# Loading and turning of the inputs put into the one order of functions, in a four-layer cross-attention kernel

## The chip, the cores and the metric

One core of one Trainium2 chip runs the kernel. The metric is the device time of one execution in microseconds (us); the time before is the median of three runs.

## The reference

```python
# x (8, 256, 256), ctx (8, 64, 128), position ids (1, 256), token types (8, 256), media mask (8, 64)
x = L0(x, ctx, W_mem, W_gate, b_gate, norm_w)          # fuse: x attends to ctx @ W_mem.T, a gate, rms norm
x = L1(x, ctx, token types, positions, weights)        # two experts, 16 heads
x = L2(x, ctx, media mask, weights)                    # gated cross attention and gelu feed-forward
x = L3(x, ctx, token types, positions, weights)        # as L1, other weights

# L1 and L3:
vm[:, :-1] = (types[:, :-1] == 1) & (types[:, 1:] == 1)
h = rms_norm(x); mixed = where(vm, h @ v_qkv, h @ l_qkv)
q, k, v = heads(split(mixed)); q, k = apply_rotary(q, k, position_ids)
c = causal_attention(q, k, v); x = x + where(vm, c @ v_dense, c @ l_dense)
x = x + cross_attention(rms_norm(x) @ cq_w, ctx @ ckv_w) @ cdense_w
m = rms_norm(x)
x = x + where(vm, silu(m @ v_gate) * (m @ v_up) @ v_down, silu(m @ l_gate) * (m @ l_up) @ l_down)
```

## The kernel before

x stays on chip for all four layers, transposed: `x_all` holds, for each of the eight batch elements, 256 features (two times 128 partitions) by 256 tokens. The work is cut into small functions, each for one batch element e and for one engine: `f_scores`, `f_turn`, `f_context`, `f_gate`, `f_sum`, `f_spread` are TensorE's (PE's) parts of the fuse layer; `n0_*` is the norm ahead of q, k, v; `q`, `k`, `v`, `first_scores`, `second_scores`, `values` are attention; `crs_*` and `cross_*` the cross attention; `up`, `down` the feed-forward; `a_*` and `b_*` the third layer. Elements 8 to 15 are the same eight in the last layer. A table of times (`put(time, stage)` and a start for each element) is sorted once, and every engine walks that one order and calls its own functions; a wait on another engine's semaphore stands at the head of a function. `f_scores(0)` is such a function for element 0.

Ahead of that order there is a block of its own, the first `with nc.Block()` (lines 746 to 887):

- SyncE (SP) issues the loads of the constants (line 749), W_mem, ctx, W_gate and the eight x (750 to 754), then waits until VectorE (DVE) has made the flags and copied the table of positions, and issues the first layer's weights (`load_mot`, `load_mot_ff`, lines 696 to 719, 19 transfers).
- ScalarE (ACT) issues position ids, token types, media mask and fourteen vectors, and copies the even ones of sixteen results from PSUM (line 779).
- DVE makes one-hot rows of the positions (793 to 800), the flags `is_vis`, `media_neg` and `early` (804 to 813), and copies the odd results (818).
- GpSimd (POOL) fills constants and zeroes pads (822 to 836).
- PE waits for the constants and for W_mem, ctx and W_gate together (`w0_in`, 48), then turns W_mem (848), ctx (851) and W_gate (856), makes two 512-column products (861), turns the vectors (871), makes the table of cosines and sines (867) and turns the eight x (877, four transposes each).

The block ends for every engine when all engines have ended it. The second block then starts, PE's part with

```python
                has_early = [pe.value_load(early[0:1, e:e + 1]) for e in range(B)]
```

(line 1031), which reads eight flags into registers; `q`, `k`, `v`, `dense`, `up` and `down` branch on them. `f_memory` (1346) takes four banks for its four products, and `f_scores` (1354) waits for nothing in the first four elements. Position and one-hot rows lie in the room of `qkv`, token types in that of `gate_w` and `up_w`, so the weights can't be loaded before they are used. x waits in the room of `wq` and `wkv`.

## Time and profile before

| | us |
|---|---|
| runs, median (lowest to highest) | 1487.04 (1486.95 to 1488.25) |
| the profiled execution | 1488.56 |
| its span | 1486.7 |
| PE busy | 1399.6 (94%) |
| DVE busy | 802.2 (54%) |
| ACT busy | 494.3 (33%) |
| POOL busy | 353.1 (24%) |
| mean granted clock of PE | 0.968 |

The span is what the profile shows from the first to the last instruction; the rest of the profiled execution's own time lies around it. The busy time of PE counts a matmul as long as it takes, at whichever of its two clocks; a granted clock of 1.00 is 2.4 GHz, 0.50 is 1.2 GHz, and a mean between them says for how much of a stretch each was granted. The order of the stages in time is: the first block, the fuse layer, the first expert layer (its attention from some 100 us on), the third layer (from some 600), and the last layer (from some 980).

### The profile page before, as it was taken

What the parts mean: (1) busy time and instruction counts of PE and PEld (TensorE: products, weight loads), DVE (VectorE), ACT (ScalarE), POOL (GpSimd) and SP (SyncE); (2) the same over time, 40 slices, a digit from 0 to 9 for tenths busy, and PEclk for the clock granted to TensorE, in tenths of its full rate; (3) what the DMA queues carried; (4) which work ended last, traced back from release to release, by engine and by line L of the source; (5) the groups of instructions that cost most, each with busy time, mean ns of one, the idle gap of its engine ahead of it and who ended that gap; (6) DMA issues with size and microseconds to landing.
All of it is one profiled execution on the core that took longest, in us unless ns stands there. A gap on an engine that the chain in (4) does not pass through costs nothing.

```text
span 1486.7 us, 27033 instructions
## 1 busy us (share of the span) xinstructions
PE 1399.6 (94%) x11507; PEld 1128.6 (76%) x11507; DVE 802.2 (54%) x1494; ACT 494.3 (33%) x835; POOL 353.1 (24%) x382
## 2 busy tenths in 40 slices
PE   3997899999999999999999999988799999999997
PEld 2786577877777778888888888876578787787776
DVE  3255666756766755543233332325585676765653
ACT  1241334233233232343445334513333323423321
POOL 1033432331322121110111101214223233232110
PEclk8797999999999999999999999988899999999999
DMA  8101000000001001110000000020000000000000
GB/s 263 44 1 57 2 1 2 2 1 2 2 2 43 2 5 51 47 49 1 1 1 0 1 0 1 0 77 1 2 2 9 2 8 9 2 8 2 8 9 15
DMA packets 19761, 27.36 MB, mean 18 GB/s; under 512 B 3416, under 2 KB 15408, under 8 KB 19376
## 3 DMA queue, kind: packets, MB, share of 16 engines
q1 hardware_dynamic: 18864, 24.20, 4.9%
q8 instruction: 103, 1.69, 0.5%
q10 hardware_dynamic: 768, 1.26, 0.3%
q14 instruction: 26, 0.21, 0.0%
HBM read 23.35 MB, written 2.10 MB: 17 GB/s over the span
## 4 chain that ended last, share of the span: by engine, by line
PE 84%; DVE 8%; ACT 2%; issue 2%; POOL 1%; DVEq 0%; POOLq 0%; ACTq 0%
PE bank L1299 13%; PE bank L1324 8%; PE bank L1187 6%; PE bank L1045 5%; PE bank L1515 4%; PE row_banks L1422 4%; PE bank L1522 4%; PE bank L1479 4%; PE row_banks L1170 4%; PE row_banks L1137 3%; PE bank L1038 2%; PE bank L1106 2%; PE row_banks L1451 2%; PE row_banks L1376 2%; PE row_banks L1142 2%; PE bank L1266 2%
## 5 line engine op out<-in xcount | busy, mean ns | idle before, releaser
L1636 ACT ACTIVATE room<-bank 128x256 f32<-128x256 f32 x176 | 66.7, 384 | 230.7 <-PE bank L1299 186.9
L956 POOL TENSOR_SCALAR_AFFINE_SELECT room<-room 128x1024 f32<-128x1024 f32 x64 | 72.3, 1130 | 274.6 <-ACT room L1606 274.6
L1299 PE MATMUL bank<-room,gate_w 128*128 128x256 f32 (+1 forms) x640 | 134.0, 332 | 3.7 <-DVE room L1877 2.5
L1324 PE MATMUL bank<-room,down_w 128*128 128x256 f32 (+1 forms) x704 | 134.6, 336 | 2.5 <-DVE room L1877 2.5
L1790 DVE TENSOR_REDUCE room<-row_banks 128x4 f32<-128x512 f32 (+1 forms) x128 | 116.5, 953 | 29.2 <-PE row_banks L1142 28.0
L1299 PE MATMUL bank<-room,up_w 128*128 128x256 f32 (+1 forms) x640 | 130.9, 327 | 0.0
L1606 ACT ACTIVATE room<-row_banks 128x1536 f32<-128x1536 f32 x64 | 92.9, 1452 | 109.9 <-PE row_banks L1170 109.9
L1324 PEld LDWEIGHTS bank<-room,down_w 128*128 128x128 f32 x704 | 108.5, 191 | 20.5 <-issue 6.9
L1874 DVE SCALAR_TENSOR_TENSOR room<-room,bank 128x256 f32<-128x256 f32 x176 | 73.4, 417 | 91.0 <-ACT room L1636 90.6
L1299 PEld LDWEIGHTS bank<-room,gate_w 128*128 128x128 f32 x640 | 99.6, 190 | 23.8 <-issue 9.9
L1299 PEld LDWEIGHTS bank<-room,up_w 128*128 128x128 f32 x640 | 103.0, 191 | 8.3
L1804 DVE RECIPROCAL room<-bank 128x256 f32<-128x256 f32 x32 | 56.1, 1752 | 43.2 <-PE bank L1187 43.2
L1877 DVE TENSOR_TENSOR room<-room,bank 128x256 f32<-128x256 f32 x176 | 74.1, 421 | 6.0
L1750 DVE SCALAR_TENSOR_TENSOR room<-x_all,vec_t,room 128x256 f32<-128x256 f32 x128 | 72.5, 627 | 1.7
L1170 PE MATMUL row_banks<-room 32*128 32x256 f32 (+1 forms) x1024 | 63.5, 364 | 9.7 <-DVE room L1797 6.8
L1045 PE MATMUL bank<-room,qkv 128*128 128x256 f32 x256 | 69.9, 422 | 0.0
L1170 PEld LDWEIGHTS row_banks<-room 32*128 32x128 f32 x1024 | 49.2, 194 | 26.6 <-issue 14.3
L922 POOL TENSOR_TENSOR room<-room 128x256 f32<-128x256 f32 x32 | 23.3, 727 | 194.3 <-ACT room L1616 194.3
L1515 PE MATMUL bank<-room,up_w 128*128 128x256 f32 x256 | 64.1, 395 | 1.9 <-issue 1.9
L1137 PE MATMUL row_banks<-room 32*128 32x128 f32 (+1 forms) x1024 | 60.0, 348 | 4.5 <-DVE room L1790 4.5
L1522 PE MATMUL bank<-room,down_w 128*128 128x256 f32 x256 | 61.9, 381 | 0.0
L1422 PE MATMUL row_banks<-room,wq 128*128 128x256 f32 x256 | 61.7, 384 | 0.0
(230 smaller groups left out, 2653.3 us busy)
## 6 DMA issues: line engine op xcount, KB each, us to landing
out_x<-wq SPq DMA_DIRECT2D x8, 256.0 KB, 2.1
qkv<-in_L_xattn_v_qkv SPq DMA_DIRECT2D x2, 768.0 KB, 4.3
qkv<-in_L_xattn_l_qkv SPq DMA_DIRECT2D x2, 768.0 KB, 6.0
gate_w<-in_L_xattn_v_gate SPq DMA_DIRECT2D x2, 640.0 KB, 6.9
gate_w<-in_L_xattn_l_gate SPq DMA_DIRECT2D x2, 640.0 KB, 7.8
up_w<-in_L_xattn_v_up SPq DMA_DIRECT2D x2, 640.0 KB, 6.4
up_w<-in_L_xattn_l_up SPq DMA_DIRECT2D x2, 640.0 KB, 7.1
down_w<-in_L_xattn_v_down SPq DMA_DIRECT2D x2, 640.0 KB, 7.0
```

The costliest lines, as they stand in the source:

```text
L1045: pe.matmul(out[:, t * S:(t + 1) * S], w[:, 1, k, at + t * P:at + (t + 1) * P], y_l[:, k, :], start=(t == k == 0), stop=False, skip_group_ ...
L1137: pe.matmul(row_banks[:, j, P * i:P + S * i], q_one[e % 2][par][r, t, i * P:(i + 1) * P], k_one[e % 2][par][r, t, 0:P * (i + 1)], start=(i ...
L1170: last = pe.matmul(row_banks[:, j, S * i:S + P * i], k_one[e % 2][par][r, t, i * P:(i + 1) * P], q_one[e % 2][par][r, t, i * P:S], start=( ...
L1187: last = pe.matmul(att_bank[32 * j:32 * j + 32, at + i * P:at + S], half if of_sums else v_pad[e % 2][:, i, 8 * t + 2 * j + par, :], probs ...
L1299: last = pe.matmul(b[:, j * S + lo:j * S + hi], w[:, k, f * P:(f + 1) * P], y[:, k, lo:hi], start=(k == 0), stop=(k == KT - 1))
L1324: last = pe.matmul(ff_bank[0][:, t * S + lo:t * S + hi], down_w[:, f, t * P:(t + 1) * P], hid[:, f, lo:hi], start=(i == t == 0), stop=(i = ...
L1422: last = pe.matmul(row_banks[:, u, j * S:(j + 1) * S], wq[:, k, at:at + P], a_y[:, k, :], start=(k == 0), stop=(k == KT - 1))
L1515: last = pe.matmul(ff_bank[(u + 1) % 2][:, j * S:(j + 1) * S], w1[:, k, at:at + P], b_y[:, k, :], start=(k == 0), stop=(k == KT - 1))
L1522: last = pe.matmul(crs_bank[:, t * S:(t + 1) * S], w2[:, k, t * P:(t + 1) * P], b_hid[:, k, :], start=(k == t == 0), stop=(k == GT - 1), s ...
L1606: act.activation(probs[w % 2], row_banks[:, :, 0:3 * P], ACT.Exp).then_inc(*ATT_ACT.does(e, f"exp{w}"))
L1790: last = dve.tensor_reduce(dst, row_banks[:, :, P * i:P + S * i], X, ALU.max, negate=True)
L1877: dve.tensor_tensor(hid[:, FF_ORDER[i], :], tanh_b[:, i % 2, :], b[:, S:2 * S], ALU.mult)\
```

## The change

The first block is gone. What must come first stands ahead of each engine's walk; turning and copying x, the vectors, positions and flags are functions of the order (`x_turn`, `x_out`, `p_vec`, `p_vec_out`, `p_one_hot`, `p_trig`, `p_trig_out`, `p_seen`), with counts of their own in a new section "x" of semaphores, and whoever reads a load waits for it. In detail:

- SP's constants are loaded in two parts, 128 columns first and the other 660 after x; W_gate gets a semaphore of its own (`wg_in`). The weights wait for POOL's pads alone, which POOL zeroes first.
- ACT issues positions and vectors first, copies three results, and only then issues media mask and token types. All eight x are copied by ACT.
- Position rows lie in the room of `prob_rows`, token types and their comparison in that of `q_all` and `k_all`, no longer in the weights' room.
- `f_memory` uses two banks in turn and waits for the copies; the eight register loads stand in `q(0)`.
- The table of times is another throughout: all stages of all layers have new times and starts.

```diff
-        with nc.Block() as block:
-            @block.sync
...
-                sp.wait_ge(pads_zero, 3)
-                sp.wait_ge(pro_dve, DVE_FIRST)
-                sp.wait_ge(*evacuated("trig"))
-                load_mot(sp, mot_w[0], True)
...
             @block.tensor
             def _(pe):
-                has_early = [pe.value_load(early[0:1, e:e + 1]) for e in range(B)]
+                pe.wait_ge(const_in, 16)
+                pe.wait_ge(w0_in, 32)
+                for t in range(KT):
+                    last = pe.transpose(all_banks[0][:, t * P:(t + 1) * P], w_mem_rows[:, t, :], ident)
...
+                pe.wait_ge(pro_act, 1)
+                pe.wait_ge(pro_dve, 1)
+                for t in range(KT):
+                    pe.matmul(all_banks[2 + t], w_mem_t[:, t * P:(t + 1) * P], ctx_t[:], start=True, stop=True).then_inc(pro_pe, 1)
+                pe.wait_ge(wg_in, 16)
...
+                has_early = []
+
+                def x_turn(e):
+                    pe.wait_ge(x_in[e], 16)
+                    if e >= 2:
+                        pe.wait_ge(*X_ACT.did(e - 2, "x"))
+                    else:
+                        pe.wait_ge(*((pro_act, 3), (pro_dve, 3))[e])
...
                 def q(e):
+                    if e == 0:
+                        pe.wait_ge(*X_DVE.did(0, "early"))
+                        has_early.extend(pe.value_load(early[0:1, b:b + 1]) for b in range(B))
...
                 def f_memory(e, i):
-                    pe.matmul((att_bank, crs_bank, *ff_bank)[i][:, 0:D], ctx_t[:, 2 * i * M:2 * (i + 1) * M], w_mem_t,
+                    if i < 2:
+                        pe.wait_ge(*(X_ACT.did(0, "half"), X_DVE.did(0, "trig"))[i])
+                    else:
+                        pe.wait_ge(*F_ACT.did(0, f"m{i - 2}"))
+                    pe.matmul(f_mem_bank[i % 2][:, 0:D], ctx_t[:, 2 * i * M:2 * (i + 1) * M], w_mem_t,
...
                 def f_scores(e):
                     if e >= FS:
                         pe.wait_ge(*F_DVE.did(e - FS, "y"))
+                    else:
+                        pe.wait_ge(pro_act, 3)
+                        pe.wait_ge(pro_dve, 3)
+                    pe.wait_ge(*X_ACT.did(e, "x"))
...
             @block.scalar
             def _(act):
...
+                act.wait_ge(pro_pe, 5)
+                act.copy(w_gate_t[:, 0:2, :], two(att_bank[:])).then_inc(pro_act, 1)
+                act.dma_start(media_u8[:], media_d.rearrange("b m -> (b m)").partition_broadcast(P)).then_inc(media_in, 16)
+                act.dma_start(type_i, type_d.rearrange("b n -> (b n)").partition_broadcast(P)).then_inc(type_in, 16)
+
+                def x_out(e):
+                    act.wait_ge(*X_PE.did(e, "x"))
+                    act.copy(x_of(e), two(x_bank[e % 2][:])).then_inc(*X_ACT.does(e, "x"))
...
             @block.sync
             def _(sp):
+                sp.dma_start(const[:, 0:P], const_d[:, 0:P]).then_inc(const_in, 16)
...
+                sp.dma_start(const[:, P:C_END], const_d[:, P:C_END]).then_inc(table_in, 16)
+                sp.wait_ge(pads_zero, 3)
+                load_mot(sp, mot_w[0])
+                load_mot_ff(sp, mot_w[0])
```

Of the table, the new part for what had been the first block (times are the table's own unit, only their order counts):

```diff
+    put(-20549.8448, "x_out")
+    put(-1254.5657, "x_turn")
...
+    put(126.2479, "p_one_hot")
+    put(126.4868, "f_mem", 0)
+    put(129.8263, "p_trig")
+    put(135.5925, "f_mem_out", 0)
+    put(147.7945, "p_seen")
+    put(161.3695, "p_trig_out")
...
+LOAD_STARTS = [-532.462, -287.087, 150.884, 171.195, 367.450, 608.477, 685.585, 1377.342]
```

How the order moves is shown at three places, all of PE. A row is a line of the kernel, an operation, destination and sources, its shape and how many follow each other. The first place is the passage from the turning of x to the fuse layer. Before (L877 turns x, L1354 is `f_scores`, L1346 `f_memory`):

```order
L877 MATMUL bank<-const,wkv 128x128 x16
L746 UNCONDITIONAL_BRANCH
L1029 UNCONDITIONAL_BRANCH
L1031 TENSOR_LOAD early x8
L1354 MATMUL row_banks<-room,x_all 128x64 x8
L1346 MATMUL bank<-room,ctx_t 128x256
```

Now (L945 turns x, L951 the vectors, L1297 is `f_scores`, L1285 `f_memory`, L959 the table of cosines and sines):

```order
L945 MATMUL bank<-const,wq 128x128 x12
L951 MATMUL bank<-const,vec_rows 128x24
L945 MATMUL bank<-const,wq 128x128 x4
L945 MATMUL bank<-const,wkv 128x128 x12
L1297 MATMUL row_banks<-room,x_all 128x64 x4
L945 MATMUL bank<-const,wkv 128x128 x4
L1285 MATMUL bank<-room,ctx_t 128x256
L1297 MATMUL row_banks<-room,x_all 128x64 x4
L959 MATMUL bank<-room,const 128x256 x4
```

The block's end and the register loads are gone from there, `f_scores(0)` comes ahead of the last x, and the table of positions behind `f_scores(1)`.

The second place is the end of the fuse layer. Before (L1376 is `f_gate`, L1057 a sum of squares, L1062 a spreading, L1045 the first half of `q(1)`):

```order
L1376 MATMUL row_banks<-x_all,room 128x256 x2
L1376 MATMUL row_banks<-wq,room 128x256 x2
L1057 MATMUL bank<-mean_w,room 128x1 x2
L1062 MATMUL bank<-const,room 128x128 x2
L1057 MATMUL row_banks<-mean_w,wq 128x1 x4
L1062 MATMUL row_banks<-const,room 128x128 x4
L1045 MATMUL bank<-room,qkv 128x256 x4
```

Now (L1319, L987, L992 and L975 are the same four; L968 is the second half of `q(1)`):

```order
L1319 MATMUL row_banks<-x_all,room 128x256 x2
L1319 MATMUL row_banks<-wq,room 128x256 x2
L975 MATMUL bank<-room,qkv 128x256 x4
L978 COMPARE_AND_BRANCH
L968 MATMUL bank<-room,qkv 128x192 x4
L978 UNCONDITIONAL_BRANCH
L968 MATMUL bank<-room,qkv 128x64 x4
L987 MATMUL row_banks<-mean_w,wq 128x1 x4
L992 MATMUL row_banks<-const,room 128x128 x4
```

`q(1)` has moved from behind the sums and spreadings of elements 6 and 7 to ahead of them.

The third place is the first attention of the last layer, element 8. Before (L1142 ends a `first_scores`, L1155 is `turn_max`, L1170 `second_scores`, L1057 and L1062 the norm's sum and spreading for element 10):

```order
L1142 MATMUL row_banks<-causal,ident_bf 128x2x128 x4
L1057 MATMUL bank<-mean_w,room 128x1 x2
L1062 MATMUL bank<-const,room 128x128 x2
L1137 MATMUL row_banks<-room 128x128 x4
L1137 MATMUL row_banks<-room 128x256 x4
L1142 MATMUL row_banks<-causal,ident_bf 128x2x128 x4
L1155 MATMUL bank<-const,room 128x128 x4
L1170 MATMUL row_banks<-room 128x256 x4
L1170 MATMUL row_banks<-room 128x128 x4
L1045 MATMUL bank<-room,qkv 128x256 x4
```

Now (L1465 is `b_down(7)`, the last product of the third layer; L1090 `turn_max`, L1105 `second_scores`):

```order
L1077 MATMUL row_banks<-causal,ident_bf 128x2x128 x4
L987 MATMUL bank<-mean_w,room 128x1 x2
L1465 MATMUL bank<-room,down_w 128x256 x4
L992 MATMUL bank<-const,room 128x128 x2
L1465 MATMUL bank<-room,down_w 128x256 x2
L1090 MATMUL bank<-const,room 128x128 x4
L1465 MATMUL bank<-room,down_w 128x256 x2
L1105 MATMUL row_banks<-room 128x256 x4
L1105 MATMUL row_banks<-room 128x128 x4
L1465 MATMUL bank<-room,down_w 128x256 x8
```

The eight pieces of `b_down(7)`, which stood ahead of `q(9)` and of all this attention, now lie inside it, and `q(10)` has moved behind the last `second_scores` of the element.

## Rows read from the trace of the kernel before

**Rows 1.** The page's first part: busy us, share of the span, instructions.

```profile
PE 1399.6 (94%) x11507; PEld 1128.6 (76%) x11507; DVE 802.2 (54%) x1494; ACT 494.3 (33%) x835; POOL 353.1 (24%) x382
```

**Rows 2.** Stretches: bounds, length, busy time by engine, granted clock, DMA share, GB/s.

```profile
0.00:24.30 24.30, 11.26 (x59) 8.93 (x59) 12.59 (x21) 5.41 (x11) 4.35 (x13) 1.00 0.69 206
24.30:39.90 15.60, 0.05 (x1) 0.00 (x1) 0.69 (x1) 0.24 (x1) 0.00 (x0) 0.61 1.06 366
39.90:93.60 53.70, 51.72 (x251) 42.62 (x251) 23.16 (x69) 16.40 (x41) 7.43 (x10) 0.83 0.05 14
93.60:150.00 56.40, 48.24 (x328) 38.65 (x332) 27.23 (x53) 17.21 (x35) 19.67 (x21) 0.85 0.10 38
200.00:625.00 425.00, 416.83 (x3952) 334.40 (x3945) 280.30 (x517) 129.39 (x229) 112.50 (x118) 1.00 0.04 12
625.00:967.00 342.00, 341.99 (x1800) 285.49 (x1799) 118.89 (x224) 147.38 (x226) 54.98 (x63) 1.00 0.03 8
967.00:1080.00 113.00, 94.07 (x869) 71.69 (x870) 52.47 (x86) 32.83 (x50) 34.69 (x35) 0.86 0.08 26
```

**Rows 3.** Pieces of the chain of waits: start, us, what.

```profile
36.76 3.17 issue
...
53.66 6.01 PE row_banks L1376 x16
...
60.25 3.65 PE row_banks L1376 x16
63.91 0.58 PE row_banks L1361 x4
...
82.02 1.84 PE row_banks L1354 x16
...
93.57 1.92 PE bank L1045 x8
...
707.35 1.92 PE bank L1522 x8
```

**Rows 4.** PE's loads of the flags: ns (min/median/max), first and last start us.

```profile
L1031 PEldq TENSOR_LOAD <-early x8: 300/302/492, 36.8 to 39.6; - x8
```

**Rows 5.** SyncE's queue, first and last issue of the first layer's weights.

```profile
21.69 0.37 SPq L696 DMA_DIRECT2D qkv<-in_L_xattn_v_qkv  x1
...
34.68 1.68 SPq L719 DMA_DIRECT2D down_w<-in_L_xattn_l_down  x1
```

**Rows 6.** PE's timeline up to 24: start, us, line, what, idle before.

```profile
12.69 0.66 PE L848 MATMUL row_banks<-const,wo 128*128 128x128 f32 x2 [12.69 <-DMA wo<-in_L_xattn_W_gate]
...
18.86 1.99 PE L867 MATMUL bank<-qkv,const 128*128 128x256 f32 x8
20.69 1.91 PE L877 MATMUL row_banks<-const,wq 128*128 128x128 f32 x16
```

**Rows 7.** DMA issues: destination, source, queue, KB each, us from issue to landing.

```profile
out_x<-wq SPq DMA_DIRECT2D x8, 256.0 KB, 2.1
...
gate_w<-in_mask_BxS_ik ACTq DMA_DIRECT2D x1, 1024.0 KB, 8.3
...
wo<-in_ctx SPq DMA_DIRECT2D x1, 256.0 KB, 9.0
```

**Rows 8.** ScalarE's timeline: one copy of a turned x.

```profile
21.33 0.59 ACT L779 COPY x_all<-row_banks 128x512 f32<-128x512 f32 x1 [1.95 <-PE row_banks L877]
```

**Rows 9.** VectorE while it works on the flags: bounds, length, busy, clock, DMA.

```profile
9.50:15.50 6.00, 5.94 (x7) 1.00 1.10 346
```

**Rows 10.** PE in two stretches: bounds, length, busy, granted clock, DMA.

```profile
112.00:124.00 12.00, 8.39 (x43) 0.72 0.18 55
1004.00:1020.00 16.00, 11.69 (x98) 0.68 0.00 1
```

**Rows 11.** PE's timeline, attention of elements 0 and 1: start, us, what, idle before.

```profile
180.83 1.35 PE L1170 MATMUL row_banks<-room 32*128 32x256 f32 x16 [2.54 <-DVE room L1797]
...
193.30 1.15 PE L1256 MATMUL row_banks<-room 32*128 32x256 f32 x16 [1.65 <-ACT room L1606]
```

More of the change, by code:

```diff
@@ L163, with load_stages, put @@
 }
+def load_stages():
+    at = []
+    def put(time, stage, *which):
+        at.append((time, stage, *which))
+    put(-20549.8448, "x_out")
+    put(-1254.5657, "x_turn")
+    return at
 def fuse_stages():
@@ L169, in put @@
         at.append((time, stage, *which))
[L171 to L188 removed]
+    put(-341.7036, "f_shift")
+    put(-341.5645, "f_scores")
+    put(-336.0780, "f_sums")
+    put(-331.9937, "f_exp")
+    put(-331.1692, "f_turn")
+    put(-325.8930, "f_turn_out")
+    put(-324.7497, "f_context")
+    put(-289.2517, "f_context_out")
+    put(-284.2985, "f_gate")
+    put(-279.0903, "f_tanh")
+    put(-270.5548, "f_gated")
+    put(-263.6497, "f_add")
+    put(-238.3910, "f_square")
+    put(-238.2306, "f_rstd")
+    put(-234.6741, "f_sum")
+    put(-233.2090, "f_mean")
+    put(-226.3863, "f_spread")
+    put(-220.9190, "f_y")
     return at
@@ new lines, in vectors, with trig @@
+                def vectors(e):
+                    pe.wait_ge(vec_in, 16 * N_VEC)
+                    pe.transpose(ff_bank[0][:, 0:KT * len(VECS)], vec_rows[:], ident[0:KT * len(VECS), 0:KT * len(VECS)])\
+                      .then_inc(*X_PE.does(e, "vec"))
+                def trig(e):
+                    pe.wait_ge(*X_DVE.did(e, "one1"))
+                    for f in range(2):
+                        for t in range(TT):
+                            at = C_TRIG + 256 * t + 128 * f
+                            last = pe.matmul(ff_bank[1][:, f * S:(f + 1) * S], const[:, at:at + P], one_hot[:, t, :],
+                                             start=(t == 0), stop=(t == TT - 1))
+                    last.then_inc(*X_PE.does(e, "trig"))
@@ L1524, in b_down @@
                     last.then_inc(*B_PE.does(e, f"down{k}"))
-                walk(order, {"f_mem": f_memory, "f_scores": f_scores, "f_turn": f_turn, "f_context": f_context,
+                walk(order, {"x_turn": x_turn, "p_vec": vectors, "p_trig": trig, "f_mem": f_memory, "f_scores": f_scores, "f_turn": f_turn, "f_context": f_context,
                              "f_gate": f_gate, "f_sum": f_sum, "f_spread": f_spread, "n0_sum": n0_sum,
@@ L1646, in f_mem_out @@
                     act.wait_ge(*F_PE.did(e, f"m{i}"))
[L1647 removed]
+                    act.copy(f_mem[:, i, :], f_mem_bank[i % 2][:, 0:D])\
                        .then_inc(*F_ACT.does(e, f"m{i}"))
```

794 lines of the change are left out of this document (374 added, 420 removed).

## The prediction

> **What bounds the kernel now.** Read the page's busy line first [rows 1]: TensorE (PE) is busy 1399.6 of 1486.7 us, so PE is the bound. What can be won is of two kinds: time in which PE idles (87.1 us) and time in which it works at 1.2 GHz instead of 2.4, which I count as busy time x (1 - mean granted clock). The table by stretch says where both lie [rows 2]. Before 24.3 PE idles 13.0 us; from 24.3 to 39.9 all of the time; from 39.9 to 93.6 only 2.0, but at a mean clock of 0.83, which loses 51.7 x 0.17 = 8.8; from 93.6 to 150 it idles 8.2 and loses 7.2; from 967 to 1080 it idles 18.9 and loses 13.2. From 200 to 625 it idles 8.2, from 625 to 967 never.
>
> Next see how the gap of 15.6 us comes about. In the chain of waits its last piece is 3.17 us of "issue" from 36.76 on, before the first matmul of the fuse stage at 39.93 [rows 3]. The eight loads of the flags `early` into PE's registers lie there, 302 ns each, from 36.8 to 39.6 [rows 4]. And before 36.76? PE has turned the last x near 24.3, but SyncE issues the first layer's weights from 21.69 to 34.68 + 1.68 = 36.36 [rows 5]. The first block ends when every engine has ended, so its barrier waits for a queue whose data nobody needs before q(0) at 93.57 [rows 3].
>
> **The change, part by part.** Times are of the profiled execution (1488.56 us); the median of the runs is 1.5 under it.
>
> *Start.* PE now waits for the constants' first 64 of 394 KB, W_mem and ctx, no longer for W_gate, whose landing released it at 12.69 [rows 6]. ctx is queued ahead of W_gate and took 9.0 us from its issue [rows 7]; I put its landing 2 us ahead of W_gate's, at 10.7, with 1 MB of token flags and 330 KB more constants beside it, which now come later. From below, 256 KB landed 2.1 us after issue where nothing else moved [rows 7], 6.9 sooner: 3.8. Between 3.8 and 10.7 I take 8, nearer to the loaded row, since 2 MB of x still come behind. The work up to the end of the two 512-column matmuls lasted from 12.69 to some 18.7 (the vectors' turning and the table's matmuls follow it [rows 6]) and is the same: 6.0, so 14.0. ScalarE then copies a bank (0.59 [rows 8]), issues two DMAs (0.9) and makes all eight copies of x alone. f_scores(0) stands behind x_turn(6), which needs x_out(4): five copies of 0.59 + 0.1, one turning of 1.91 / 4 = 0.48. Sum 14.0 + 1.5 + 3.4 + 0.5 = **19.4 against 39.93**.
>
> *Fuse stage up to q(0).* Before, 39.93 to 93.57 holds 53.6 - 2.0 idle - 8.8 clock = 42.8 us of work at full speed. After, two f_scores (0.92 each) and one f_turn (0.58) [rows 3] come behind q(0), and one x_turn (0.48) and the table's matmuls (1.99 [rows 6]) join: 42.8 again. The register loads are moved to just ahead of q(0) and stay exposed, from 36.8 to 39.9 before: +3.1. The stage begins with two batch elements in flight, not four, so its links over ScalarE, VectorE and GpSimd are covered less: 6 us idle against 2.0, a choice. Clock: I allow 2. q(0) comes at 19.4 + 42.8 + 3.1 + 6 + 2 = 73.3 instead of 93.57, and 2.4 us of work are left over: **18 us won** by then.
>
> What hides the flags? VectorE's work on them takes 5.94 us [rows 9] and now lies between f_sums(1) and f_gated(0). f_sums(1) ends near 26, f_gate(0), 3.65 at full speed [rows 3], near 32: just covered, if the token flags have landed. If not, f_gated(0), the table's copy and, behind that, f_mem(1) are late next.
>
> *Weights.* SyncE passes no wait on the flags any more and issues them near 11 instead of 21.69. At the 366 GB/s of the gap [rows 2] 6.6 MB take 18 us, so they are in by 31, long before q(0). Worth nothing, and by themselves they cost nothing.
>
> *The order table.* All the rest is sorted anew. Two places matter. From 112 to 124, the end of the fuse stage, PE is busy 8.39 of 12 us at a clock of 0.72 [rows 10]: 3.6 idle, 2.3 lost. Now q(1), about as long as q(0), stands ahead of f_sum(6) and fills the wait for GpSimd's sum. I take 5 of the 5.9. Against it, q(2) no longer stands between the first two second_scores of element 0, so the exponentials show; the nearest row is 1.65, the wait of the cross attention's second product for them [rows 11]; I take 1.7. From 1004 to 1020, the start of the last layer, PE is busy 11.69 of 16 at 0.68 [rows 10]: 4.3 idle, 3.7 lost. There b_down(7), eight pieces of 0.96 (two took 1.92 [rows 3]), now stands inside the attention chain of element 8. I take 6 of the 8. In the steady stretches I take 0, between -5 and +5.
>
> Sum: 18 + 5 - 1.7 + 6 = 27. Profiled 1461.3, **median 1460**.
>
> One rule can be weighed here. The row shows 302 ns for a register load and 3.1 us for the eight with their edges. The Trainium skill (DMA: Bandwidth & Descriptors, "Latency and other measured facts") gives about 600 ns as the floor of a tensor load; eight would be 4.8 us and the gain 1.7 smaller. The row is of this very instruction, so it decides.
>
> **Rivals.** (a) *The forecast*, 0.62: 1450 to 1470.
>
> (b) *Late flags and a half clock*, 0.15. ScalarE issues the 1 MB of token flags near 14.6, while SyncE pushes 6.6 MB of weights into the same engines. Under load they took 8.3 [rows 7]: 23. Served only behind the weights they land near 33, VectorE has done with them at 39, and f_gated(0) is 6 us late with nothing else for PE to do: 6 lost. For it: from 24.3 to 39.9 the DMA share is 1.06. Against: they come from two queues, and they landed under load before. The clock: before, the first f_gate took 6.01 instead of 3.65 [rows 3]; if thin work keeps PE at 1.2 GHz through the first gates, up to 9 more are lost. Both: 27 - 15 = 12 won, 1475. The Trainium skill (TensorE: Matmul & The Clock Gate, "What's actually happening") has an idle TensorE at 1.2 GHz by default. The page of the profile grants 1.00 before the first matmul, so there the two differ; either way it is the same in both kernels.
>
> (c) *More*, 0.15: PE starts at 4, loses no clock, bubbles stay at 2, and the table gives 5 more: 40 won, 1447.
>
> (d) *Slower*, 0.04. The new table puts a wait into the elements of the steady stretches, since feed-forward pieces are spread otherwise between the links of attention. The price is 2.54 us, PE's wait for VectorE before a second_scores where nothing else stands ready [rows 11]. There are 24 elements (8 in each of three layers): from 1.1 us each on the gain is gone, at 2.54 it is 61 - 27 = 34 slower, 1521. Against it: 625 to 967 has no idle time to spare and each chain still has other pieces between its links.
>
> (e) *The barrier isn't what holds PE*, 0.04: the gap is the transfers', and PE would wait for them without a barrier too. Then only the table acts, between 10 won and nothing. Against it: what follows the gap is a register load, and f_scores reads nothing of this layer's weights.
>
> **How the numbers follow.** About 0.2% (3 us) is what a measurement of this kernel can tell from no change. Faster are (a), (b), (c) and half of (e): 0.94; within 0.2% 0.02; slower 0.04. The range goes from just under (c) to (b): 1446 to 1475. Left out are (d), (e) and the tails, under 0.2 together.
>
> **What would show it.** Right: the first matmul at 4 to 11 and the first f_scores at 17 to 22; no hole in PE's work over 4 us behind it; the weights issued from about 11; the register loads as one hole of 2.5 to 3.5 us just ahead of q(0), which begins at 67 to 79; the mean clock above 0.9 in the 20 us after q(1) and around the first attention of the last layer. Wrong: a hole near 35 to 45 that VectorE's flags end, or a mean clock under 0.8 from the first f_scores to 45 (b); idle time over 15 us in the 425 us that answer to 200 to 625 (d); PE still idle some 15 us before the first f_scores (e).

## The result, and the profile after

| | before | after |
|---|---|---|
| median of the runs, us | 1487.64 (1486.95 to 1488.86, 4 runs) | 1439.49 (1438.18 to 1446.08, 4 runs) |
| profiled execution, us | 1488.56 | 1439.24 |
| its span, us, and mean granted clock | 1486.7, 0.968 | 1437.5, 0.985 |

The ratio is 0.9685, 95% interval 0.967 to 0.970: 48 us faster. The forecast was 1460 with a range of 1446 to 1475, so the sign was right and the size was not: 27 us forecast, 48 won. Of the cases, (c), "more", came nearest (its four reasons add up to 42 us won, not the 40 that it states); which of them acted is told below.

The runs of one kernel differ in their mean granted clock (of after, three stand at 0.985 or 0.986 and 1438.2 to 1439.8 us, one at 0.977 and 1446.1), so small differences below are read between runs of equal clock.

The page's first part, after [rows 1]:

```profile
PE 1383.1 (96%) x11507; PEld 1116.1 (78%) x11507; DVE 791.9 (55%) x1490; ACT 501.0 (35%) x845; POOL 349.7 (24%) x382
```

PE's idle time fell from 87.1 to 54.4 us. The stretches of the kernel after, cut where the program begins `f_scores(0)`, `q(0)`, `first_scores(0,0)`, a point in the attention of element 1, the third layer's `a_q(0)`, the end of its `b_project`, and so on (bounds, length, PE busy, granted clock, DMA share, GB/s) [rows 2]:

```profile
0.00:19.30 19.30, 11.47 (x48) 1.00 0.94 298
19.30:65.30 46.00, 43.23 (x245) 1.00 0.37 124
65.30:97.10 31.80, 29.56 (x166) 0.95 0.07 21
97.10:172.00 74.90, 58.77 (x671) 0.89 0.05 21
172.00:554.00 382.00, 378.89 (x3737) 1.00 0.04 11
554.00:928.80 374.80, 374.80 (x2003) 1.00 0.03 10
928.80:1035.00 106.20, 93.52 (x893) 0.89 0.09 28
1035.00:1392.00 357.00, 354.76 (x3507) 1.00 0.02 6
1392.00:1437.50 45.50, 38.05 (x254) 1.00 0.04 12
```

Beside the same stretches of before, with the clock's loss as busy time x (1 - clock), the loss of the first stretch left out because little works there:

| stretch | length before, after | PE idle before, after | clock's loss before, after |
|---|---|---|---|
| start to `f_scores(0)` | 39.9, 19.3 | 28.6, 7.8 | |
| to `q(0)` | 53.6, 46.0 | 2.0, 2.8 | 8.8, 0 |
| to `first_scores(0,0)` | 30.3, 31.8 | 3.7, 2.2 | 2.9, 1.5 |
| attention of elements 0, 1 | 76.2, 74.9 | 12.9, 16.1 | 8.2, 6.5 |
| steady, to `a_q(0)` | 388.2, 382.0 | 8.2, 3.1 | 0, 0 |
| third layer | 377.8, 374.8 | 0, 0 | 0, 0 |
| start of the last layer | 114.0, 106.2 | 18.9, 12.7 | 12.4, 10.3 |
| steady | 360.0, 357.0 | 4.8, 2.2 | 0, 0 |
| end | 46.7, 45.5 | 8.0, 7.5 | 0.8, 0 |

Idle time gives 32.7 of the 49.2 us by which the span is shorter, the clock 14.8. The start is the largest line, 20.6 us, and every line but one gives something. Of the 3.0 of the third layer, where PE never idles, some 1.5 are seven 256-column products of the expert layers' gate and `up` weights (L1299 before, 40 of them in this stretch; L1234 after, 33) that the table moved across the cut; the rest isn't placed. PE's timeline in the kernel after, at four places (start, us, line, what, idle before) [rows 6]:

```profile
6.67 0.66 PE L920 MATMUL row_banks<-const,wo 128*128 128x128 f32 x2 [6.67 <-DMA wo<-in_ctx]
...
9.06 3.75 PE L928 MATMUL row_banks<-ctx_t,room 128*128 128x512 f32 x4 [0.88 <-DVE ctx_t L1711]
...
19.27 1.00 PE L1297 MATMUL row_banks<-room,x_all 128*128 128x64 f32 x8
...
65.28 1.97 PE L975 MATMUL bank<-room,qkv 128*128 128x256 f32 x8 [0.62 <-issue]
```

`f_scores(0)` was forecast at 19.4 and begins at 19.27, with nothing idle between it and `q(0)` for more than 0.74 us. The register loads [rows 4], and SyncE's first and last weight issue [rows 5]:

```profile
L1015 PEldq TENSOR_LOAD <-early x8: 295/304/496, 62.1 to 64.8; - x8
```

```profile
8.79 0.43 SPq L716 DMA_DIRECT2D qkv<-in_L_xattn_v_qkv  x1
...
28.75 1.57 SPq L739 DMA_DIRECT2D down_w<-in_L_xattn_l_down  x1
```

The loads lie from 62.1 on, while matmuls that were queued ahead of them still run: PE stops for 0.62 us only. The weights are issued from 8.79, past everything.

### The profile page after: what moved, and what is told of

It reads as the page before. It is cut to its first block, busy times and chain, and to the rows that moved or that the text cites. A ratio compares the mean times of both kernels' runs of the same rounds, so it can differ in the third digit from the quotient of the medians.

```text
span 1437.5 us, 27076 instructions
## 1 busy us (share of the span) xinstructions
PE 1383.1 (96%) x11507; PEld 1116.1 (78%) x11507; DVE 791.9 (55%) x1490; ACT 501.0 (35%) x845; POOL 349.7 (24%) x382
## 4 chain that ended last, share of the span: by engine, by line
PE 90%; DVE 4%; ACT 2%; issue 1%; POOL 1%; DMA 0%; SPq 0%; POOLq 0%; ACTq 0%; DVEq 0%
PE bank L1234 15%; PE bank L1259 8%; PE bank L1122 6%; PE bank L975 5%; PE bank L1458 4%; PE row_banks L1105 4%; PE bank L1465 4%; PE row_banks L1365 4%; PE bank L1422 4%; PE row_banks L1072 4%; PE bank L1040 3%; PE bank L968 3%; PE row_banks L1077 2%; PE row_banks L1394 2%; PE row_banks L1319 2%; PE bank L1201 2%
## 5 line engine op out<-in xcount | busy, mean ns | idle before, releaser
L1811 DVE TENSOR_REDUCE room<-row_banks 128x4 f32<-128x512 f32 (+1 forms) x128 | 116.7, 954 | 46.7 <-PE row_banks L1077 46.5
L1234 PE MATMUL bank<-room,gate_w 128*128 128x256 f32 (+1 forms) x640 | 135.9, 335 | 5.1 <-DVE room L1898 2.2
L1895 DVE SCALAR_TENSOR_TENSOR room<-room,bank 128x256 f32<-128x256 f32 x176 | 73.3, 417 | 107.1 <-ACT room L1606 106.9
L1234 PE MATMUL bank<-room,up_w 128*128 128x256 f32 (+1 forms) x640 | 130.9, 327 | 0.0
L1259 PE MATMUL bank<-room,down_w 128*128 128x256 f32 (+1 forms) x704 | 128.5, 332 | 0.0
L1234 PEld LDWEIGHTS bank<-room,gate_w 128*128 128x128 f32 x640 | 98.5, 190 | 32.2 <-issue 18.0
L1234 PEld LDWEIGHTS bank<-room,up_w 128*128 128x128 f32 x640 | 103.0, 191 | 8.3
L1898 DVE TENSOR_TENSOR room<-room,bank 128x256 f32<-128x256 f32 x176 | 74.1, 421 | 6.0
L1105 PE MATMUL row_banks<-room 32*128 32x256 f32 (+1 forms) x1024 | 63.8, 365 | 10.6 <-DVE room L1818 5.9
L1105 PEld LDWEIGHTS row_banks<-room 32*128 32x128 f32 x1024 | 49.4, 195 | 26.6 <-issue 16.8
L975 PE MATMUL bank<-room,qkv 128*128 128x256 f32 x256 | 61.5, 383 | 0.6 <-issue 0.6
L1767 DVE SCALAR_TENSOR_TENSOR room<-x_all,vec_t,room 128x256 f32<-128x256 f32 x128 | 60.4, 533 | 1.9
L1422 PE MATMUL bank<-room,wo 128*128 128x256 f32 x256 | 59.3, 380 | 0.0
```

The costliest lines, as they stand in the source:

```text
L975: pe.matmul(out[:, t * S:(t + 1) * S], w[:, 1, k, at + t * P:at + (t + 1) * P], y_l[:, k, :], start=(t == k == 0), stop=False, skip_group_ ...
L1105: last = pe.matmul(row_banks[:, j, S * i:S + P * i], k_one[e % 2][par][r, t, i * P:(i + 1) * P], q_one[e % 2][par][r, t, i * P:S], start=( ...
L1234: last = pe.matmul(b[:, j * S + lo:j * S + hi], w[:, k, f * P:(f + 1) * P], y[:, k, lo:hi], start=(k == 0), stop=(k == KT - 1))
L1259: last = pe.matmul(ff_bank[0][:, t * S + lo:t * S + hi], down_w[:, f, t * P:(t + 1) * P], hid[:, f, lo:hi], start=(i == t == 0), stop=(i = ...
L1422: last = pe.matmul(crs_bank[:, t * S:(t + 1) * S], wo[:, k, t * P:(t + 1) * P], a_context[:, k, :], start=(k == t == 0), stop=(k == GT - 1 ...
L1811: last = dve.tensor_reduce(dst, row_banks[:, :, P * i:P + S * i], X, ALU.max, negate=True)
```

## Experiments

Times are medians, with the lowest and highest in brackets; "after" is the changed kernel, 1439.5. The kernel before was measured again beside each group of experiments (medians 1487.4 to 1488.3).

### The frame and the table apart

The change has two halves: the frame (one block, x and flags as functions, loads awaited by readers) and the order table. The first kernel has the frame of after and the table of before, with the x functions in their old order:

```
-    each(LOAD_STARTS, load_stages())
+    for b in range(B):
+        order.append((-500.0 + 2 * b, "x_turn", b))
+        order.append((-499.0 + 2 * b, "x_out", b))
...
-FUSE_STARTS = [463.491, 468.887, 566.857, 569.780, ...]
+FUSE_STARTS = [71.942, 97.642, 152.609, 175.010, ...]
```

> The changed kernel's frame (no block of its own, loads awaited by readers, one walk) with the table of before; the eight turnings of x, the vectors and the positions stand ahead of the table's first entry, the flags behind f_sums(1). Theory A, the frame carries most: the first f_scores moves from 39.9 to about 21, the half clock of 39.9 to 58 is gone (8.8 us), register loads cost under 1: 27 to 30 us faster than before, 1458 to 1461. Theory B, the table carries most: under 16 us faster (the idle gap alone at best), 1472 or more.

Measured: 1466.1 (1465.7 to 1469.3), 22 us faster than before: between the two theories. `f_scores(0)` came at 21.34, as theory A had it; 5 to 8 us of the rest are missing. The second has the frame of before and the table of after, without its x functions:

> The kernel of before with the changed kernel's table (without the entries of x, vectors, positions, flags). The gap and the barrier stay. Theory A: what the traces differ by behind q(0), 7.7 us of steady idle time, 8.3 at the start of the last layer, 1.3 at the end, some 1 between: 16 to 20 us faster, 1468 to 1472. Theory B: 30 or more faster, 1458 or less. If frame and table help each other, the two gains together stay under 48.

Measured: 1471.3 (1470.8 to 1472.8), 17 faster, theory A. Apart they give 39, together 48, so 9 us come only from the two together. The traces show two places. In the kernel with the old table, VectorE and PE between 25 and 35:

```profile
25.81 1.22 DVE L1725 TENSOR_SCALAR room<-room 128x2048 f32<-128x2048 int32 x1
27.01 0.07 DVE L1727 MEMSET is_vis<- 128x8 bf16 x1
27.11 2.29 DVE L1729 TENSOR_TENSOR is_vis<-room 128x2040 bf16<-128x2040 f32 x1
...
30.11 1.73 DVE L1735 TENSOR_REDUCE early<-is_vis 1x8 int32<-1x1536 bf16 x1
31.77 0.27 DVE L1898 TENSOR_REDUCE room<-row_banks 128x2 f32<-128x128 f32 x1
```

```profile
33.15 2.07 PE L1300 MATMUL row_banks<-wo,room 64*128 64x256 f32 x4 [4.91 <-ACT wo L1615]
35.15 2.07 PE L1308 MATMUL row_banks<-x_all,room 128*128 128x256 f32 x4
37.02 1.91 PE L1308 MATMUL row_banks<-wq,room 128*128 128x256 f32 x4
38.73 1.79 PE L1308 MATMUL row_banks<-x_all,room 128*128 128x256 f32 x4
```

The flags stand ahead of the soft maximum of element 2 (L1898), ScalarE and then PE wait for it, 4.91 us, and the pieces behind the hole take about twice the 1.03 to 1.13 us of a gate piece elsewhere. In the kernel with the old frame and the new table, PE in the fuse stage behind the gap:

```profile
40.00:60.00 20.00, 18.43 (x75) 0.66 0.08 25
60.00:75.00 15.00, 14.26 (x59) 0.63 0.00 1
```

Here the clock loses 18.43 x 0.34 + 14.26 x 0.37 = 11.5 us; from `f_scores(0)` to `q(0)` it takes 55.9 us (39.21 to 95.06), in the kernel after 46.0 with the same order of these functions. So each half alone pays a price in the fuse stage that isn't there with both.

### The flags in the old table, moved alone

```
+    move([("p_seen", 0)], ("f_gated", 0))
```

> The new frame with the old table (1466.1), and one entry of it moved: VectorE's work on the flags stands ahead of f_gated(0), behind the soft maximum of elements 2 and 3. Theory A: the flags were in the way of f_shift(2), for which ScalarE waited 6.2 us and PE 4.91, and the half clock behind that hole stretched four pieces from 1.13 and 1.03 to 2.07, 2.07, 1.91 and 1.79, 3.5 us more; moved, they lie beside f_gate(0) and (1): 1457.5 to 1461.5. Theory B: another wait takes the hole's place (f_gated(0) now has the flags ahead of it, and only two gates cover them): 1464 to 1467.

Measured: 1462.3 (1459.7 to 1462.6), just above theory A's range. The hole of 4.91 is gone from the trace and `first_scores(0,0)` comes at 96.9 instead of 105.4, 8.5 earlier, as theory A had it; but only 4 to 6 us are left of that at the end. From 110 to 120 PE is then busy 7.24 us at a clock of 0.50. The cause of the hole is shown; its worth at the end is about half of what the place itself shows.

### The barrier and the queue

```
-                load_mot(sp, mot_w[0], True)
-                load_mot_ff(sp, mot_w[0])
...
+                load_mot(sp, mot_w[0], True)
+                load_mot_ff(sp, mot_w[0])
                 w = mot_w[1]
```

The kernel before, with the first layer's weights issued behind the barrier instead of ahead of it:

> The kernel of before with one edit: SyncE issues the first layer's weights at the start of the second block, so the barrier has no queue to wait for. Theory A, the barrier waits for SyncE: PE starts f_scores about 28 (24.9 + 3.2) and not 39.9, 11 to 12 us earlier, and if the idle time of 4 us is too short to lower the clock, 8.8 more: 1467 to 1476. Rival: the gap has another cause (PE's own start of a block, or data): f_scores stays at 37 or later, within 3 us of 1487.

Measured: 1474.7 (1470.9 to 1482.0), 13 faster, theory A. PE's first piece behind the barrier, in its trace:

```profile
28.47 3.65 PE L1352 MATMUL row_banks<-room,x_all 128*128 128x64 f32 x16 [4.17 <-issue]
```

The gap of 15.6 us has shrunk to the register loads, and `f_scores(0)` comes 11.5 us earlier. So it was the queue of issues that the barrier waited for, not the data: SyncE now issues the weights from 25.31 to 41.30, mostly behind PE's start. The runs differ by their clock: 1470.9 at 0.978, 1482.0 (the profiled one) at 0.968.

### What a gap costs

```
                 has_early = []
+                pe.wait_ge(mot_ff_in, 16 * MOT_FF_DMAS)
```

> The changed kernel with one added wait: PE's first turning of x waits until all weights of the first layer have landed (about 32). It makes a gap like that of before without a block. Theory A, a gap costs its length and the clock behind it: PE idle from 14.4 to about 32, 17 us, and a clock near 0.5 for some 18 us behind it, 8 to 9 more: 1464 to 1467. Rival, the fuse stage had its half clock for another reason (thin work at the end of the first block, the barrier): 17 us alone, 1455 to 1458.

Measured: 1464.3 (1462.8 to 1466.5), 25 slower than after. In its trace:

```profile
36.99 2.97 PE L946 MATMUL bank<-const,wq 128*128 128x128 f32 x12 [23.11 <-DMA down_w<-in_L_xattn_l_down]
...
88.78 1.97 PE L976 MATMUL bank<-room,qkv 128*128 128x256 f32 x8 [0.64 <-issue]
```

PE was idle for 23.1 us and `q(0)` comes 23.5 later than in after. From its `f_scores(0)` at 42.75 to `q(0)` are 46.0 us, as in after: the gap costs its length and about 1 us of clock (the turnings of x behind it take 5.8 us instead of 4.8 up to `f_scores(0)`).

The time lies in theory A's range, but by luck: the weights landed at 37 and not at 32, so the gap was 6 us longer than forecast, and of the 8 to 9 us of half clock forecast behind it only about 1 came. What the rival says of the clock is nearer: a gap of this length doesn't by itself bring 8 us of half clock. Behind it stand the turnings of x, almost without a pause; behind the gap of the old frame with the new table came the thin first links of the fuse stage, with a pause of 1.43 us, and there 11.5 us were lost. The runs of each kernel agree (mean clock 0.974 to 0.977 here, 0.968 or 0.969 there). Whether it is the thin work that makes the difference wasn't tested.

### Parts of the table

```
+    move([("b_down", 7, k) for k in range(8)], ("first_scores", 8, 0))
+    move([("b_gelu", 7, 2), ("b_gelu", 7, 3)], ("q_mask", 8))
```

> The changed kernel (1439.5) with the eight b_down(7) put back ahead of first_scores(8,0), and with them ScalarE's last two b_gelu(7) ahead of q_mask(8). Theory A: these eight pieces of 0.96 us are what covers the attention of element 8 in the changed table; without them the pieces of idle time of before come back there (1.03, 0.52, 1.92, 0.84 between 1004 and 1013) with the half clock around them, 6 to 8 us: 1445.5 to 1447.5. Theory B: another part of the table (q(9), q(10), the squares) does the covering and the pieces are worth under 2 us: 1439.5 to 1441.5.

Measured: 1448.0 (1447.4 to 1453.9), 8.5 slower. The idle time comes back where it was expected:

```profile
970.40 0.43 PE L1002 MATMUL bank<-const,room 128*128 128x128 f32 x2 [1.03 <-POOL room L817]
972.19 1.09 PE L1100 MATMUL bank<-const,room 128*128 128x128 f32 x4 [1.35 <-DVE room L1821]
974.12 1.66 PE L1115 MATMUL row_banks<-room 32*128 32x256 f32 x16 [0.84 <-DVE room L1828]
977.44 1.67 PE L1115 MATMUL row_banks<-room 32*128 32x256 f32 x16 [1.66 <-ACT room L1586]
```

Around them (965 to 985) PE is busy 14.72 of 20 us at 0.74; in after (961 to 981) 19.31 of 20 at 1.00. That is 4.6 + 3.8 = 8.4: theory A, half a us above its range.

```
+    move([("q", 1)], ("v", 1))
```

> The changed kernel with q(1) moved back behind f_spread(7), so that nothing stands ahead of f_sum(6). Theory A: q(1) covers the wait for GpSimd's sums, and the 3.6 us of idle time and 2.3 of clock of before between 112 and 124 come back: 1443.5 to 1445.5. Theory B: in the changed kernel f_sum(6) waits 1.30 us with q(1) ahead of it, so q(1) covers only as much as it is long, and what stands behind it (v(1), first_scores) waits for nothing new: the wait grows by 2.5 to 3 and nothing else, 1442 to 1442.5. Theory C, the place doesn't matter: 1438.5 to 1440.5.

Measured: 1447.7 (1444.6 to 1451.8), 8.2 slower by the medians. At an equal clock the difference is smaller: the profiled run, 1449.6, has a clock of 0.977, and three runs of after at 0.977 stand at 1446.1 to 1446.4; the fastest are 1444.6 (0.980) here and 1438.2 (0.986) in after. So 3.2 to 6.4. The waits for GpSimd's sums in the trace:

```profile
94.47 0.61 PE L996 MATMUL row_banks<-mean_w,wq 128*128 128x1 f32 x4 [2.25 <-POOL wq L884]
...
96.48 0.60 PE L996 MATMUL row_banks<-mean_w,wq 128*128 128x1 f32 x4 [1.41 <-POOL wq L884]
```

The profile of the repetition of after (below) has the same clock up to here and `q(0)` at the same time. In it one wait of 1.30 stands there, and from 71 to `first_scores(0,0)` PE idles 2.2 us; here 5.2, and `first_scores(0,0)` comes 3.35 later (105.89 against 102.54). No half clock is added. In this pair, then, theory B is right: the wait grows by 3 us and nothing else. The 6.4 of the fastest runs leave theory A's 4 to 6 possible in others.

```
+    move([("q", 2)], ("second_scores", 0, 1))
```

> The changed kernel with q(2) moved back between second_scores(0,0) and second_scores(0,1). Theory A: it fills the 1.66 us in which PE waits there for the exponentials, and the clock in 108 to 120 (mean 0.6) rises: 1.7 to 3 us less, 1436.5 to 1437.8. Theory B: the wait is only moved, since q(2) is missing where it stood, behind second_scores(0,3), and the next pieces wait for the exponentials: 1439 to 1440.5.

Measured: 1438.5 (1437.6 to 1446.7), and once more:

> The changed kernel with q(2) back between second_scores(0,0) and (0,1), once more. The first five runs gave 1437.6 to 1438.5 where the mean clock was 0.986, and the changed kernel 1438.2 to 1439.8 at 0.985 and 0.986. Theory A: it is 1 to 1.5 us faster at equal clock: its runs at 0.985 or above lie at 1437 to 1438.6. Theory B: no difference: they lie between 1438 and 1440.

1441.3 (1438.1 to 1446.8). At 0.986 its runs lie at 1437.6 to 1438.5, those of after at 0.985 and 0.986 between 1438.2 and 1439.8. In its trace the wait of 1.66 us is gone, and `values(0)` waits 1.49 and 0.68 instead, for VectorE and GpSimd; the clock from 110 to 120 is 0.66 instead of 0.52. By these runs it gains 0.3 us (those at 0.986 alone) to 0.9 (all of them), and the medians don't resolve it: neither theory is shown.

```
+    for e in (1, 9):
+        move([("q", e + 2)], ("second_scores", e, 1))
+        move([("n0_y", e + 2)], ("cross_shift", e - 1))
```

> The changed kernel with q(3) and q(11) put between the first two second_scores of elements 1 and 9 (with VectorE's n0_y ahead of cross_shift, which they need). Theory A: they fill the waits of 1.03 and 1.04 us there; behind cross_second, where they stood, cross_values then waits for its exponentials, 0.5 or so: 1 to 2 us less in all, 1437.5 to 1438.5. Theory B: VectorE's two or three extra operations ahead of cross_shift delay the cross attention by as much as is won: 1439 to 1441.

Measured: 1449.4 (1440.7 to 1452.7); its run at 0.985 stands at 1440.7. The waits of 1.03 and 1.04 are gone, but `cross_project` now waits 1.97 us for ScalarE, twice, where `q(3)` and `q(11)` had stood. Neither theory named that wait. By the run at 0.985 the result is B's, no gain.

### The table behind the fuse stage

To tell the fuse stage's order from the rest, the two tables were spliced in the new frame, at PE's `v(3)` (the product v of element 3, at 175.9 in after) and the matching places of the other engines:

```
+UP_TO = {"pe": 117, "dve": 87, "act": 85, "pool": 42}
...
+        order += a[:n] + b[n:]
```

> The changed kernel whose table is the new one up to v(3) (on the other engines up to the same place) and the old one from there on. Theory A: the new table's gain behind that place is the sum of what the traces show there, 5.1 us of idle time in the stretch before the second layer, 2.6 in the steady stretch of the last, 7.7 to 8.3 at the last layer's start and 1.3 at the end, 17 in all: 1455 to 1459. Theory B: the rest of the table is worth only the start of the last layer (8): 1446.5 to 1449.

Measured: 1460.3 (1457.4 to 1463.2), 20.8 slower than after and 1.3 above theory A's range.

> The reverse: new frame, old table up to v(3), new table from there on. Theory A: additive with the kernel before it, 1466.1 less the same 17: 1447.5 to 1451; so the fuse stage's order is worth 8 to 11 us in the new frame. Theory B: 1457 to 1460, the rest is worth 8 only and the fuse stage's order 18.

Measured: 1446.7 (1445.3 to 1452.4), 19.4 faster than the old table in the new frame and 0.8 below theory A's range. So the order behind `v(3)` is worth 19 to 21 us and that up to there 6 to 7 in the new frame.

The traces say the same without medians. From PE's `v(3)` to the end each profile holds the same 10311 matmuls (bounds, length, PE busy, granted clock, DMA share, GB/s; before, after, the first splice, the second):

```profile
204.20:1486.70 1282.50, 1242.62 (x10311) 0.99 0.03 11
175.90:1437.50 1261.60, 1236.13 (x10311) 0.99 0.03 11
180.80:1461.40 1280.60, 1240.39 (x10311) 0.99 0.03 11
191.20:1450.70 1259.50, 1233.56 (x10311) 0.99 0.03 11
```

With the old order behind it the stretch lasts 1280 to 1283 us (1279.9 in the new frame with the old table), with the new one 1259.5 to 1261.6, whatever stands ahead of it. Between before and after, PE's idle time in it falls from 39.9 to 25.5, 14.4 of the 20.9; the rest is a shorter busy time of the same matmuls, of the clock and otherwise.

The same mark tells where frame and table help each other. In the new frame the profiled runs reach `v(3)` at 184.2 with the old table and at 175.9 with the new one; in the old frame at 204.2 and at 208.6. So ahead of `v(3)` the new order wins 8 us in one frame and loses 4 in the other, and behind it it wins about 20 in both. (The repetition of after at the lower clock, below, is there at 184.4: in such a run the 8 us are gone.)

Of the 20, the start of the last layer is 8. Of the other 12, 8.2 are small waits, nearly all in the steady stretches; these are four of the rows of before between 200 and 588:

```profile
297.90 2.44 PE L1324 MATMUL bank<-room,down_w 128*128 128x256 f32 x12 [0.51 <-DVE room L1877]
332.89 0.94 PE L1137 MATMUL row_banks<-room 32*128 32x128 f32 x16 [1.50 <-DVE room L1790]
...
390.60 0.94 PE L1137 MATMUL row_banks<-room 32*128 32x128 f32 x16 [1.09 <-DVE room L1790]
...
449.56 2.54 PE L1045 MATMUL bank<-room,dense 128*128 128x256 f32 x8 [2.07 <-DVE room L1819]
```

In after the longest between 172 and 554 is 0.46.

### Covers of the start

```
                     act.dma_start(pos_i, ...).then_inc(pos_in, 16)
+                    act.dma_start(type_i, ...).then_inc(type_in, 16)
+                    act.dma_start(media_u8[:], ...).then_inc(media_in, 16)
...
-                sp.dma_start(const[:, 0:P], const_d[:, 0:P]).then_inc(const_in, 16)
+                sp.dma_start(const[:], const_d).then_inc(const_in, 16)
```

> The changed kernel with the whole table of constants loaded first again and with the token types and media flags issued right behind the positions on ScalarE's queue, as before. Theory A: what let PE start at 6.7 instead of the forecast 8 is the lighter traffic ahead of ctx; with 330 KB and 1 MB more beside it ctx lands near 9 to 10.5, and all that follows up to q(0) is 2.5 to 4 us later: 1442 to 1443.5. Theory B: the flags, which then land by 12, let VectorE do them sooner, and this makes up for it; or ScalarE's table load sets the start (its first copy runs at 8.08): under 1.5 us.

Measured: 1445.2 (1443.4 to 1453.0), 5 to 6 slower, above theory A's range.

```profile
11.65 0.66 PE L920 MATMUL row_banks<-const,wo 128*128 128x128 f32 x2 [11.65 <-DMA wo<-in_ctx]
```

PE starts 5 us later than in after: ctx lands 9.8 us after its issue instead of 4.8. Theory A had it landing at 9 to 10.5, and `q(0)` (69.79) is 4.5 later. The earlier flags don't make up for it. Which of the two loads holds ctx up, the rest of the constants ahead of it or the flags beside it, isn't separated.

```
+                    dve.tensor_reduce(spare[:, 0, :], is_vis[0:1, :, 0:LATE], X, ALU.max)
```

(three of them):

> The changed kernel with three more reductions of the flags (1.73 us each, 5.2 in all, written to a spare tile) ahead of the one that counts. Theory A: VectorE's flags are just covered by the first eight pieces of f_gate, so everything longer shows: they end at 35.6 instead of 30.4, f_gated(0) and with it f_shift(2) and f_sum(0) come 3.5 us later, PE idles that much at 35 to 40 and may fall to half clock behind it, as in the kernel with the old table: 3.5 to 8 us slower than the unchanged one. Theory B: there is spare cover, or the loss is made up again before q(0): under 1 us.

Measured: 1441.9 (1439.8 to 1448.3); its runs at 0.985 stand at 1439.8 and 1440.3, 0.5 to 1 above those of after. VectorE ends the flags at 34.8 instead of 30.5, and one new hole opens:

```profile
35.48 0.70 PE L1286 MATMUL bank<-room,ctx_t 128*128 128x256 f32 x2 [1.48 <-DVE cos_sin L1733]
```

The flags end 4.3 us later and PE loses 1.5 there, so "just covered" was too tight: some 3 us were to spare. Theory B by the runs at 0.985; the medians, 1441.9 against 1440.5 of the repetition, lie 1.4 apart.

```
                         has_early.extend(pe.value_load(early[0:1, b:b + 1]) for b in range(B))
+                        twice = [pe.value_load(early[0:1, b:b + 1]) for b in range(B)]
```

> The changed kernel with the eight loads of the flags into PE's registers done twice ahead of q(0). Theory A: the loads run in PE's sequencer while matmuls that are queued already still run (in the trace they lie from 62.1 to 64.8, and PE stops only at 64.66, for 0.62 us); of eight more, 2.4 us, the queue hides little or nothing further, since the matmuls behind them can't be queued meanwhile: 2.4 to 2.7 us slower. Theory B: they are hidden all the same: under 0.5 us.

Measured: 1446.4 (1440.9 to 1447.6), four of five runs at 0.976 or 0.977, where after has 1446.1 to 1446.4. But the run doesn't test the theories. The first row is from its trace, the second from that of the repetition of after, which has the line once:

```profile
L1015 PEldq TENSOR_LOAD <-early x8: 295/305/495, 67.8 to 70.6; - x8
L1015 PEldq TENSOR_LOAD <-early x8: 295/302/490, 67.7 to 70.4; - x8
```

There are eight loads in both, at the same place ahead of `q(0)`, which begins at 71.06 and at 70.88:

```profile
71.06 1.97 PE L975 MATMUL bank<-room,qkv 128*128 128x256 f32 x8 [0.64 <-issue]
```

The second eight, on the next line of the kernel, aren't in the trace, and nothing reads their registers. So this is the changed kernel once more, and what further loads would cost stays open. Its slower runs say nothing of the loads either: in the profiled one the half clock, at 40 to 50, lies ahead of them.

### The changed kernel once more

> The changed kernel once more, unchanged, beside the three that follow. Its runs so far lie at 1438.2 to 1439.8 (mean granted clock 0.985) and once at 1446.1 (0.977). Theory A: the work and the waits are the same in every run and only one stretch of half clock comes or not, so the times stand in two groups some 6 to 8 us apart, each with its own mean clock, and the median depends on how many runs fall into which. Theory B: the 1446.1 was a single disturbed run; all others lie within 2 us.

Measured: 1440.5; the five runs at 1438.6, 1439.2 (clock 0.986, 0.985), 1440.5 (0.981), 1446.3 and 1446.4 (0.977). The profiled one is of the last kind, and shows what differs. PE from 40 to 52 and from 35 to 40 (PE busy, clock, DMA share, GB/s), first in the profile of after, then in the repetition:

```profile
40.00:52.00 12.00, 12.00 (x67) 1.00 0.01 3
35.00:40.00 5.00, 4.25 (x33) 1.00 0.07 21
```

```profile
40.00:52.00 12.00, 12.00 (x37) 0.50 0.01 3
35.00:40.00 5.00, 4.26 (x31) 0.97 0.08 25
```

From 40 to 52 PE is busy throughout in both, and in one at 1.2 GHz: 6 us. Before it both are alike, 9.26 us busy between 30 and 40 and one pause of 0.74 at 38. `q(0)` then begins 5.6 later. It isn't the only such stretch, as theory A had it: `v(3)` is 8.4 later (184.37 against 175.92), the further 3 us at a mean clock of 0.83 against 0.89 in the attention of elements 0 and 1, and 1.3 are made up behind it. On the two groups theory A is right, with one run in between.

## Why the prediction was off

**What bounds the kernel**: right. PE was the bound, the gap was the barrier behind SyncE's issues and then the register loads; moving the issues alone took 11.5 us of it away. Rival (e) falls.

**Start**: `f_scores(0)` forecast at 19.4, measured 19.27. That it fits so well is luck. PE's first matmul, forecast at 8 between 3.8 and 10.7, came at 6.67 (6.0 to 6.6 in the other kernels of this frame), 1.3 sooner. The work up to the end of the 512-column matmuls and the turning of W_gate, which now follows them, then took 7.8 us and not 6.0: the four matmuls of 512 columns took 3.75 (2.50 before) and waited 0.5 longer. So rival (b)'s "it is the same in both kernels", said of the clock at the start, is wrong. The rest was 0.6 shorter. The ends were not safe either: with the old traffic the first matmul is at 11.65, and the lower one, 3.8, was read from transfers that write x out.

**Fuse stage up to `q(0)`**: forecast 73.3, measured 65.28, outside the 67 to 79 that were named as the sign of being right. This is one of the two steps that failed. Three terms were too dear. "+3.1" for register loads that "stay exposed": 0.6, since they lie from 62.1 to 64.8 while PE works off queued matmuls until 64.66; before, there was no queue left behind the barrier, so the row could not show this. "6 us idle": 2.2 besides. "Clock: I allow 2": 0 in the profiled run; in the runs at 0.977 it is 6. The first two hold in every run; the third is a matter of the run.

The rule on register loads weighed there, about 600 ns each (the Trainium skill, DMA: Bandwidth & Descriptors, "Latency and other measured facts"), is not borne out: they took 304 ns, and neither price reached the path in full.

**Flags**: right that they are covered. Rival (b)'s hole appeared, but only with the old table, from VectorE's order and not from a late transfer: the token flags landed 8.4 us after issue. Its other half, a half clock through the first gates, didn't come in the profiled run; in the runs at 0.977 PE has one of 12 us behind them, 6 of (b)'s "up to 9".

**End of the fuse stage, +5**: 3.1 by the profiles of `q1_behind` and the repetition, up to 6.4 by the fastest runs; right, at most 2 too large. **`q(2)`, -1.7**: 0.3 to 0.9, right in its sign.

**Start of the last layer, +6**: 8.5 by `down7_ahead`, somewhat too small.

**"In the steady stretches I take 0, between -5 and +5"**: this is the other step that failed, and the larger. The spliced tables give 19 to 21 us behind `v(3)`, 11 to 13 of them outside the last layer's start. Of these the trace of after shows 5.1 + 2.6 + 0.5 us less idle time, 8.2; the rest isn't attributed row by row. The row of 200 to 625 with its 8.2 idle us stood in [rows 2], and a new table was free to fill them. For a table that is sorted anew, what is idle in a stretch is the first estimate of what can be won there; a symmetric error around 0 leaves it out.

The two profiled runs add up so. Up to `v(3)` 28.3 us were won (204.2 to 175.9), where 18 + 5 - 1.7 = 21.3 had been forecast; behind it 20.9, where 6 had been forecast. The first difference, 7, is nearly all the fuse stage up to `q(0)`; of the second, 15, some 2 are the last layer's start and 13 the rest. 27 + 7 + 15 make the 49 by which the span is shorter. Either failed step alone would have left the time inside the range of 1446 to 1475 (1460 less 7 or less 13); both together did not.

**Rival (d)**, waits added to the steady stretches: the opposite happened. **Case (c)**: of its reasons, idle time of 2 us and no loss of clock up to `q(0)` held in the profiled run, and the table gave more, but 13 and not 5; PE didn't start at 4.

## To carry to other kernels

A barrier at a block's end waits also for queues that only issue transfers; issue long loads behind it, or let their readers wait. Put register loads where matmuls are queued ahead of them: the eight here then cost 0.6 us instead of 3.1. When an order is sorted anew, read each stretch's idle time as what can be won, not only the stretches where the work visibly moves. Measure the halves of a change apart and together: up to `v(3)` the same new order won 8 us in one frame and lost 4 in the other. And look in the trace whether an edit is there before reading its time: an instruction whose result nobody reads may be missing.

## What the hardware showed unexpectedly

- The same program, with the same pauses, ran 12 us of solid work at 1.2 GHz in some executions and at 2.4 in others: 1438 to 1440 us or 1446. What decides it stays open. The Trainium skill (TensorE: Matmul & The Clock Gate, "What's actually happening") says that the window in which the chip looks at PE's activity "doesn't reset when your kernel starts"; differences between executions of one program would agree with that, and no run here tests it.
- A pause of 23 us cost about 1 us of clock where dense work followed (`wait_weights`), and one of 15.4 us was followed by 11.5 us of it where thin work followed (old frame, new table). Two kernels show this; that the kind of work is the cause isn't shown.
- SyncE's 19 issues of the first layer's weights took 14.7 us before (21.69 to 36.36), the longest 2.08, and a block's end waited for them: with them behind it, `f_scores(0)` came 11.5 us earlier.
- The profile grants a clock of 1.00 to the first 19 us of after, but the four matmuls of 512 columns at 9.06 took 3.75 us, and the same four took 1.96 when they began at 16.24 in the kernel with the old frame and the new table. The granted clock of the first microseconds doesn't fit these durations. They would fit what the Trainium skill (TensorE: Matmul & The Clock Gate, "What's actually happening") states, that an idle TensorE is at 1.2 GHz by default.
